# Row statistics that travel with the rows of the first expert layer, a reload through two queues, and other edits around one block boundary

## The reference

```python
x = x + 0.5 * ffn(layernorm(x), router_w, router_b, w1, w2)
x = x + mamba(layernorm(x), ...)
x = x + 0.5 * ffn(layernorm(x), router_w, router_b, w1, w2)

# layernorm: (x - mean) / sqrt(var + 1e-5) over the 128 features of a row
# ffn:   logits = h @ router_w + router_b; route = softmax(logits)
#        out = (silu(a) * g) @ w2[e] for the row's best of 8 experts e, (a, g) = split(h @ w1[e]); out * max(route)
# mamba: xc, z = split(h @ W_in); xc = silu(conv4(xc)); dt, B, C = xc @ W_x ...; state recurrence of 16 states;
#        y = (scan + xc * D) * silu(z); out = layernorm(y @ W_out) * ln_g + ln_b
```

## Time and profile before

| | |
|---|---|
| median of three runs | 426.33 us |
| profiled execution, its own time | 426.06 us |
| profiled execution, span from first to last instruction | 424.3 us |
| PE busy | 385.9 us (91%) |
| DVE busy | 314.6 us (74%) |
| ACT busy | 262.7 us (62%) |
| POOL busy | 260.5 us (61%) |
| mean granted clock of TensorE | 0.975 of full |

### The profile page before, as it was taken

One profiled execution on the slowest core, in us unless ns is written; L12 is line 12 of the kernel. 1 busy time (PEld: TensorE's weight loads), 2 busy tenths in 40 slices (PEclk: granted clock), 3 DMA queues, 4 the chain that ended last, 5 costly groups with the idle time before them and its releaser, 6 DMA issues.

```text
span 424.3 us, 8691 instructions
## 1 busy us (share of the span) xinstructions
PE 385.9 (91%) x3080; PEld 352.6 (83%) x3080; DVE 314.6 (74%) x481; ACT 262.7 (62%) x508; POOL 260.5 (61%) x187
## 2 busy tenths in 40 slices
PE   8989889996798988999999899999999888999994
PEld 8878889995664377899998789999888888989893
DVE  4854446372799699999999999999969855544551
ACT  3314244331397999999999999999545315433430
POOL 5044756664001009999999999999950054666653
PEclk9898989999699999999999999999999999999998
DMA  7918492211300164543444345444246311111110
GB/s 217 339 38 255 115 403 78 44 39 33 99 0 4 44 153 21 167 140 125 147 158 131 125 151 157 128 127 169 68 144 254 104 32 32 41 46 45 40 39 25
DMA packets 42731, 47.48 MB, mean 112 GB/s; under 512 B 13313, under 2 KB 34370, under 8 KB 42178
## 3 DMA queue, kind: packets, MB, share of 16 engines
q1 hardware_dynamic: 39746, 40.80, 31.0%
q0 software_dynamic: 2944, 6.13, 6.0%
HBM read 37.38 MB, written 9.54 MB: 111 GB/s over the span
## 4 chain that ended last, share of the span: by engine, by line
DVE 22%; ACT 22%; PE 17%; POOL 7%; issue 4%; another core or an unknown queue 1%; DMA 1%; POOLq 0%; DVEq 0%
DVE phase L969 10%; PE psum L671 9%; ACT phase L1053 8%; ACT phase L1063 7%; POOL w_sb L888 6%; PE psum L683 5%; DVE xc L1288 4%; PE psum L1186 1%; PE psum L1154 1%; ACT dt L923 1%; DVE xc L1284 1%; POOL phase L380 1%; DVE stats L269 1%; DMA phase<-token_rows,token_row 1%
## 5 line engine op out<-in xcount | busy, mean ns | idle before, releaser
L888 POOL TENSOR_TENSOR w_sb<-phase,w_sb 128x1024 f32<-128x1024 f32 x62 | 144.7, 2418 | 0.0
L969 DVE TENSOR_TENSOR_SCAN phase<-phase,psum 128x1024 f32<-128x1024 f32 x64 | 142.4, 2272 | 2.8 <-PE psum L1136 2.3
L671 PE MATMUL psum<-phase 128*128 128x128 f32 x736 | 93.2, 279 | 3.9 <-issue 3.0
L671 PEld LDWEIGHTS psum<-phase 128*128 128x128 f32 x736 | 88.3, 195 | 5.3 <-issue 3.8
L380 POOL DMA_INDIRECT phase<-token_rows,token_row x46 | 47.7, 1038 | 59.2 <-DVE token_row L484 45.8
L1053 ACT ACTIVATE phase<-dtxT,B_cols 128x256 f32<-128x256 f32 x192 | 80.0, 499 | 0.3
L1154 PE MATMUL psum<-ident,w_sb 128*128 128x128 f32 x512 | 67.5, 276 | 3.3 <-DVE silu_z L962 0.9
L1063 ACT ACTIVATE phase<-dt,neg_A 128x1024 f32<-128x1024 f32 x64 | 69.8, 1140 | 0.0
L505 DVE TENSOR_TENSOR phase<-phase,psum 128x512 f32<-128x512 f32 x46 | 31.5, 685 | 44.7 <-remote 18.0
L1154 PEld LDWEIGHTS psum<-ident,w_sb 128*128 128x128 f32 x512 | 56.4, 141 | 8.8 <-POOL w_sb L888 7.1
L568 ACT ACTIVATE phase<-psum 128x512 f32<-128x512 f32 x46 | 27.3, 593 | 52.9 <-remote 29.7
(11 more groups left out here) (180 smaller groups left out, 404.5 us busy)
## 6 DMA issues: line engine op xcount, KB each, us to landing
w_sb<-c_rows SPq DMA_DIRECT2D x32, 512.0 KB, 3.9
w_sb<-ffn_w SPq DMA_DIRECT2D x16, 512.0 KB, 7.7
B_diag<-dt SPq DMA_DIRECT2D x4, 1024.0 KB
phase<-B_diag SPq DMA_DIRECT2D x32, 128.0 KB, 3.8
token_rows<-x_tok SPq DMA_DIRECT2D x8, 264.0 KB, 4.5
w_sb<-ffn_w SPq DMA_DIRECT2D x8, 256.0 KB, 7.6
x_tok<-attn_x SPq DMA_DIRECT2D x4, 256.0 KB, 4.1
x_tok<-x_rows SPq DMA_DIRECT2D x4, 256.0 KB, 3.8
```

The source lines that it names most:

```text
L671: last = nc.tensor.matmul(psum[:, 2 * k + part, c * P:(c + 1) * P], w1_tile[:, t % W1_RING, part * F + c * P:part * F + (c + 1) * P], xsT_ ...
L888: nc.gpsimd.tensor_tensor(hC[:, k % HC_RING, :], H[:, k % H_RING, :], C_sb[:, j % C_RING, :], ALU.mult).then_inc(M["hC_ready"], 1)
L969: nc.vector.tensor_tensor_scan(H[:, k % H_RING, :], dA[:, k % DECAY_RING, :], dBx_bank[k % SLOTS], 0.0, ALU.mult, ALU.add).then_inc(M["sca ...
```

## The change

Four edits meet at the boundary. In the first expert layer `give` is followed by a `bn_stats` of the row that it has just written, into six more columns of the ring `ys_sb`, and the scatter writes 134 columns; `x_rows` and `x_tok` have 134 columns. The scatter waits for the statistics (`rows_measured`). The four loads back to `x_tok` bring 134 columns each, two issued by SP (groups 0 and 2) and two by ACT (groups 1 and 3). In the second block `bn_stats` is gone for both halves, and `norm_spread` reads the six columns in `x_tok`; each half begins with a wait for two loads. `centre_W_out` stands at the end of DVE's first block. PE's idle matmuls at the front are 6, then 3 after `var_ready`, then 2 after `shift_ready`, in place of 16 at once.

```diff
-        x_rows = nc.dram_tensor("x_rows", (N, D), F32).ap()
+        x_rows = nc.dram_tensor("x_rows", (N, D + SW), F32).ap()
...
+        def load_back(engine, g):
+            engine.dma_start(x_tok[:, g * GROUP:(g + 1) * GROUP, :],
+                             x_rows[g * CH:(g + 1) * CH, :].rearrange(by_token, p=P)).then_inc(x_back[g], 16)
...
             def scatter(t):
-                pool.wait_ge(f["ys_ready"], t + 1)
+                pool.wait_ge(finished, t + 1)
                 nc.gpsimd.indirect_dma_start(into, bass.IndirectOffsetOnAxis(ap=token_row[:, t:t + 1], axis=0),
-                                             ys_sb[:, t % YS_RING, :], None).then_inc(f["ys_stored"][t % YS_RING], 16)
+                                             ys_sb[:, t % YS_RING, 0:width], None
+                                             ).then_inc(f["ys_stored"][t % YS_RING], 16)
...
+                if arrives:
+                    dve.wait_ge(f["ys_ready"], t + 1)
+                    nc.vector.bn_stats(ys_sb[:, t % YS_RING, D:D + SW], row).then_inc(M["rows_measured"], 1)
...
                 wait_scattered(sp, FF[0])
-                for g in range(NG):
-                    sp.dma_start(x_tok[:, g * GROUP:(g + 1) * GROUP, 0:D],
-                                 x_rows[g * CH:(g + 1) * CH, :].rearrange(by_token, p=P)
-                                 ).then_inc(x_back[g], 16)
+                for g in range(0, NG, 2):
+                    load_back(nc.sync, g)
...
-                ffn_gpsimd(pool, FF[0], x_rows)
+                ffn_gpsimd(pool, FF[0], x_rows, M["rows_measured"], D + SW)
...
                 ffn_vector(dve, FF[0], landed)
+                dve.wait_ge(loaded_m, 16 * M_LOADS)
+                centre_W_out(dve)
...
                 ffn_scalar(act, FF[0], True)
+                wait_scattered(act, FF[0])
+                for g in range(1, NG, 2):
+                    load_back(nc.scalar, g)
...
                 dve.wait_ge(loaded_m, 16 * M_LOADS)
-                centre_W_out(dve)
-                landed = [(x_back[g], 16) for g in range(NG)]
-                norm_variance(dve, M["norm"], x_row, landed, batch_tiles[0])
+                dve.wait_ge(x_back[0], 16)
+                dve.wait_ge(x_back[1], 16)
+                norm_spread(dve, M["norm"], x_tok[:, batch_tiles[0], D:D + SW], batch_tiles[0])
                 norm_rstd(dve, M["norm"], batch_tiles[0], 1)
...
-                norm_variance(dve, M["norm"], x_row, landed, batch_tiles[1])
+                dve.wait_ge(x_back[2], 16)
+                dve.wait_ge(x_back[3], 16)
+                norm_spread(dve, M["norm"], x_tok[:, batch_tiles[1], D:D + SW], batch_tiles[1])
                 norm_rstd(dve, M["norm"], batch_tiles[1], 2)
...
-                keep_warm(16, 0)
+                keep_warm(6, 0)
+                pe.wait_ge(M["norm"]["var_ready"], 1)
+                keep_warm(3, 0)
+                pe.wait_ge(M["norm"]["shift_ready"], 1)
+                keep_warm(2, 0)
```

More of the change, by code:

```diff
@@ L42, in macaron_kernel @@
     RW = D + 4
+    SW = 6
     PROB, RSTD, SHIFT = D, D + 1, D + 2
@@ L102, in macaron_kernel @@
         ln_b_sb = sb("ln_b_sb", [P, D])
-        x_tok = sb("x_tok", [P, NT, RW])
+        x_tok = sb("x_tok", [P, NT, D + SW])
         xn_tok = sb("xn_tok", [P, NT * D])
@@ L178, in macaron_kernel @@
             (P, XS_RING, RW), (P, NORM_RING, D), (P, TURN_RING, P), (P, W1_RING, 2 * F), (P, 2, F), (P, U_RING, F),
-            (P, YS_RING, D),
+            (P, YS_RING, D + SW),
             (P, NT * P // 2), (P, NT * SLOT_TILES // 2), (P, NT * 2 * SLOT_TILES // 2))
@@ L269, in norm_variance, with norm_spread @@
                 last = nc.vector.bn_stats(stats[:, j, :], src(j))
-            norm_spread(dve, s, last, tiles)
-        def norm_spread(dve, s, last, tiles):
             chain(dve, last)
-            mean_even, mean_odd, diff = stats[:, tiles, 1], stats[:, tiles, 4], mean_diff[:, tiles]
+            norm_spread(dve, s, stats[:, tiles], tiles)
+        def norm_spread(dve, s, rows, tiles):
+            mean_even, mean_odd, diff = rows[:, :, 1], rows[:, :, 4], mean_diff[:, tiles]
             nc.vector.tensor_tensor(mean_sum[:, tiles], mean_even, mean_odd, ALU.add)
-            nc.vector.tensor_tensor(spread[:, tiles], stats[:, tiles, 2], stats[:, tiles, 5], ALU.add)
+            nc.vector.tensor_tensor(spread[:, tiles], rows[:, :, 2], rows[:, :, 5], ALU.add)
             chain(dve, nc.vector.tensor_tensor(diff, mean_even, mean_odd, ALU.subtract))
@@ L358, in wait_scattered, with centre_W_out @@
                 sp.wait_ge(f["ys_stored"][k], f["ys_before"][k] + 16 * ((SLOT_TILES - 1 - k) // YS_RING + 1))
+        def load_back(engine, g):
+            engine.dma_start(x_tok[:, g * GROUP:(g + 1) * GROUP, :],
+                             x_rows[g * CH:(g + 1) * CH, :].rearrange(by_token, p=P)).then_inc(x_back[g], 16)
+        def centre_W_out(dve):
+            chain(dve, nc.vector.tensor_reduce(W_mean[:], W_out_sb[:], AX.X, ALU.add))
+            chain(dve, nc.vector.tensor_scalar(W_mean[:], W_mean[:], 1.0 / D, None, ALU.mult))
+            nc.vector.tensor_tensor(W_out_sb[:], W_out_sb[:], W_mean[:].unsqueeze(2).broadcast_to([P, NH, D]),
+                                    ALU.subtract).then_inc(M["W_centred"], 1)
         def store_rows(sp, f):
@@ L364, in store_rows @@
                 sp.dma_start(token_rows[g * CH:(g + 1) * CH, :].rearrange(by_token, p=P),
-                             x_tok[:, g * GROUP:(g + 1) * GROUP, :]).then_inc(f["row_stored"], 16)
+                             x_tok[:, g * GROUP:(g + 1) * GROUP, 0:RW]).then_inc(f["row_stored"], 16)
         def ys_bank(t):
@@ L371, in xsT_bank, with ffn_gpsimd @@
             return psum[:, 7 - 3 * (t % 2), 0:P]
-        def ffn_gpsimd(pool, f, into):
+        def ffn_gpsimd(pool, f, into, finished, width):
             def gather(t):
@@ L513, in give @@
                     dve.wait_ge(f["ys_stored"][t % YS_RING], f["ys_before"][t % YS_RING] + 16 * (t // YS_RING))
-                nc.vector.scalar_tensor_tensor(out=ys_sb[:, t % YS_RING, :], in0=ys_bank(t),
+                row = ys_sb[:, t % YS_RING, 0:D]
+                nc.vector.scalar_tensor_tensor(out=row, in0=ys_bank(t),
                                                scalar=xs_sb[:, t % XS_RING, PROB:PROB + 1],
@@ L819, in macaron_kernel @@
         KB = K // B
[L821 to L826, removed]
         EARLY_STATES = 3
@@ L1036, in recurrence_vector @@
             add_rows(1)
-            norm_spread(dve, FF[1], row_stats(range(TB, NT)), ALL)
+            chain(dve, row_stats(range(TB, NT)))
+            norm_spread(dve, FF[1], stats[:], ALL)
             norm_rstd(dve, FF[1], ALL, 1)
@@ L1259, in _ @@
                 recurrence_gpsimd(pool)
-                ffn_gpsimd(pool, FF[1], out.rearrange("b l d -> (b l) d"))
+                ffn_gpsimd(pool, FF[1], out.rearrange("b l d -> (b l) d"), FF[1]["ys_ready"], D)
             @block.vector
```

2 lines of the change are left out of this document (1 added, 1 removed).

## The result

The changed kernel takes 504.56 us (median of 4 runs, 500.09 to 506.49) where the kernel before took 426.97 us beside it: ratio 1.1786, 95% interval 1.1736 to 1.1837. The change makes the kernel 78 us slower; the forecast was 424.6 us, with a range of 423.2 to 427.2.

A forecast was written before the change was run, and what follows sets the result against it. The prediction saw no engine busy throughout and judged the boundary by its chain of waits. Terms of -1.3 and -0.45 us took 426.06 to 424.3; with 0.27 for the median, 424.6 us, range 423.2 to 427.2.

The forecast's parts named there:

- The scatter waits for the statistics: First expert layer: bn_stats delays each scatter, hidden by slack in 20 of 23 tiles; the last group moves 0.31 us once.
- My worst case for this step: First expert layer: if the slack were gone in every tile, 23 x 0.31 = 7.1 us.
- The pair lands late: Rival at the boundary loads: the four mix or longer, unaligned rows cost more; up to 427.1 us; chance 0.14.
- signs of being wrong: First pair over 4 us after SP's wait, W_in records over 0.5 us each, or first layer's end moving over 0.5 us.
- T: Instant when norm_spread starts in the second block: 111.31 us before the change, forecast 110.0, 1.3 us earlier.
- End of the first layer: Last three scatters move by 0.31 us, so SP's wait was forecast to pass at 106.49 us.
- Start of the block: Two issues each on SP and ACT: second block forecast to start at 107.95 us, 0.7 earlier, if ACT's cost matches SP's.
- The landing: First pair of boundary loads: taken to land 3.5 us after SP's wait, between bounds of 2.8 and 6.0 us.
- The second half's statistics: Second block: 1.67 us of bn_stats leave DVE; chunk 1 starts at T + 11.6, gaining 0.45 us, bounds zero and 0.87.
- Sum of the front: Second block up to chunk 1: -1.3 us from T and -0.45 from the second half's statistics, -1.75 us together.
- the rival of the low clock: Front of second block: gaps in PE's idle matmuls delay full clock; 425.7 us, or 426.6 if after both heads; chance 0.20.
- Centring: Three DVE instructions, 1.07 us, move to 102.2 us behind the last give, where DVE idles; saving counted in T.

The follow-up runs named there:

- e4: Kernel before the change, with scatter and loads leaving out two columns (504-byte rows), no other edit: 503.73 us against 427.8.
- e2: Changed kernel with rows of 1024 bytes, all written, repeated writes kept: 426.06 us against 427.8 for the kernel before, one run.
- e1: Changed kernel, 536-byte rows, but every empty lane writes a spare row of its own: 430.16 us against 427.8 for the kernel before, ratio 1.0045.
- e3: Changed kernel with rows of 640 bytes, repeated writes kept: 428.20 us against 427.8 for the kernel before, one run.
- e5: The kernel of e2 again, in 12 runs: 415.85 us against 417.35 for the kernel before, ratio 0.9979.
- e12: The kernel of e2 with 16 idle matmuls at once in the front: 426.48 us against 427.95 for the kernel before, ratio 0.9977.
- e14: Changed kernel with rows of 560 bytes, all written, repeated writes kept: 501.67 us against 418.23 for the kernel before, one run.
- e13: Changed kernel with rows of 544 bytes, all written, repeated writes kept: 418.29 us against 418.23 for the kernel before, one run.
- e11: The kernel of e2 with SP issuing all four loads: 427.94 us against 427.95 for the kernel before, ratio 0.9997.

## Why the prediction was wrong

**The step that failed** is the first of the sum, "The scatter waits for the statistics". I priced the `bn_stats` there, and the wait, and never the scatter itself: 23 of them with rows of 536 instead of 512 bytes. Longer rows came up only in the loads, bounded by stores of 528-byte rows, and there no row is written again. I had also not asked which rows the empty lanes write, though `head_row` and `empty` stand in the code that the trace's gathers and scatters use. The measured size of the missing term is +78 us (e4 shows it alone: +76). The sum had the sign wrong with it: -1.75 us forecast, +78 measured.

My worst case for this step, 7.1 us, was a bound on `bn_stats` and not on the step. None of the rivals contained the mechanism. "The pair lands late" had the right cause (rows of odd length) in the wrong place. One of the signs of being wrong that I had named came plainly: the first layer's end moved by 80 us, and half a microsecond was the limit.

**The front, seen where the stalls are gone** (e2), since in the changed kernel it starts 80 us later. In the changed kernel it runs alike: `norm_spread` 4.0 us after SP's wait, products at T + 4.5 in 3.70 us, chunk 1 at T + 11.9. The rows of e2 are, in order: scatter, SP's issue, idle matmuls, `norm_spread`, turning, products, square root, second `hold`, second turning, its copy, hold of chunk 1, chunk 1:

```profile
103.09 0.97 POOL L398 DMA_INDIRECT x_rows<-phase,token_row  x1 [0.30 <-issue]
106.06 0.92 SPq L362 DMA_DIRECT2D x_tok<-x_rows  x2
108.19 5.30 PE L347 MATMUL psum<-ident 128*128 128x128 f32 x22 [6.67 <-PEq L718]
110.19 0.17 DVE L277 TENSOR_TENSOR mean_sum<-x_tok 128x8 f32<-128x8 f32 x1 [6.97 <-DMA x_tok<-x_rows]
113.33 1.11 PE L1458 MATMUL psum<-ident,xn_tok 128*128 128x128 f32 x8
114.61 3.70 PE L1468 MATMUL psum<-xnT,W_in_sb 128*128 128x512 f32 x8 [0.16 <-ACT xnT L1362]
114.96 0.30 ACT L327 ACTIVATE std<-spread,eps_sb 128x8 f32<-128x8 f32 x1
116.63 0.59 ACT L1370 COPY phase<-psum 128x512 f32<-128x512 f32 x1 [0.27 <-PE psum L1468]
119.87 1.20 PE L1458 MATMUL psum<-ident,xn_tok 128*128 128x128 f32 x8
120.51 0.58 ACT L1362 COPY xnT<-psum 128x512 f32<-128x512 f32 x1 [0.21 <-PE psum L1458]
120.99 1.02 ACT L1370 COPY phase<-psum 128x1024 f32<-128x1024 f32 x1
122.04 1.01 DVE L1301 TENSOR_SCALAR xc<-phase,conv_w_sb,conv_b_sb 128x512 f32<-128x512 f32 x2 [0.28 <-ACT phase L1370]
```

- *End of the first layer*: forecast +0.3 us; SP's wait passes at 106.06 instead of 106.18. In e1 and e3 it passes at 109.2 and 109.3 with the same instructions, so that one trace can't size this term.
- *Start of the block*: forecast 107.95 with ACT's issues at SP's price; 108.19, although ACT's two issues took only 1.02 us and the wait passed 0.4 us earlier than forecast. The block starts 1.1 us behind the last issue and not 0.45; what sets that isn't shown, and it is on no chain.
- *T*: forecast 110.0, measured 110.19, released by the loads and not by the block's end, as forecast. The landing was mis-sized: 4.1 us after the wait instead of 3.5 (3.95 to 4.2 in e1, e3, e5 and e12), at the limit of 4 us that I had set for being wrong. The earlier end of the first layer made up for most of it; that T comes within 0.2 us is luck. In e14's one run it was 5.4 us, late as in the rival; why isn't shown.
- *The second half's statistics*: chunk 1 was forecast at T + 11.6 and starts at T + 11.85, against 12.06 before: a gain of 0.2 us instead of 0.45. The second `hold` ends at T + 7.0, as forecast (T + 6.9). What I missed is PE: the second turning stands behind the `W_in` products for `z` and starts at 119.87, and ACT, done with its eight tiles at 120.30, waits for it until 120.51.
- *Sum of the front*: chunk 1 at 122.04 instead of 123.37, -1.33 us against -1.75. The mechanism was right and the size off by a quarter; in the time it isn't clear of the spread (e5).
- *The clock*: the rival of the low clock didn't come in e2, and its premise was wrong. I took 6 records in a microsecond from a window, where a record that reaches over an edge counts in both; PE's 32 records from 108.65 took 5.84 us, most of them at half clock. The six idle matmuls last until about 110.8 and not 109.8 (12 records took 2.90 us in e14), so the gap of 1.0 us doesn't open: in e2 PE is busy without a gap from 108.19 on. The granted clock is 0.50 until 113.2 us and 1.00 behind it, and `W_in`'s eight records took 3.70 us, the same as before. In e1 the rival came in part. The idle matmuls start at 111.66, PE has no gap either, and the clock is 0.50 until about 117.6. The turning takes 1.61 us instead of 1.11, the products start at T + 5.1 instead of T + 4.4, and chunk 1 at T + 12.6 instead of T + 11.85. The rise comes 5.1 us behind the block's start in e2, 5.9 in e1 and 4.2 in the kernel before, so one good trace doesn't settle this rival.
- *Centring* cost nothing where it went, as forecast.

**Order of the evidence.** e4 shows the loss in the kernel before, e1 removes it from the changed kernel without touching the row's length, and e13 and e14 switch it by 16 bytes. That a partial write is done as a read and a write, one after the other, is my reading of it; the runs show the three conditions (a length with a remainder by 32, one row, many lanes) and not what the memory does.

## What to carry to other kernels

When a row that is scattered gets longer or shorter, check that its bytes are a multiple of 32, and which rows the padding lanes write. If both are bad, each repeated write cost about 0.09 us here, and the gathers issued behind it came late. Padding the row is the cheap repair: 544 or 576 bytes in place of 536.

## What the runs showed of the hardware

- Rows whose length isn't a multiple of 32 bytes, written again by many lanes of a scatter: 850 such writes cost 76 to 83 us (504 bytes +75.9, 536 bytes +77.6, 560 bytes +83.4). With 536 bytes the DMA engines count as busy all the time from 60 to 90 us while they move 125 GB/s, and for a tenth of the time from 120 to 150 us.
- Full rows of 1024 bytes, twice as many bytes as 512, scattered by 23 instructions, cost nothing that can be measured (ratio 0.9979 with the rest of the change, 0.9942 to 1.0017).
- Two queues that load at once: `norm_spread` starts 3.95 to 4.2 us after the wait in all of e1, e2, e3, e5 and e12, and 4.0 us with one queue (e11).
